# Odd chunks of a state-space kernel's scores with their source halves exchanged between the column halves of TensorE

## What is computed

```python
a = -jax.nn.softplus(A_log).transpose(0, 2, 1)
Lm = jnp.exp(segsum(a))                       # decay from s to l, zero for s > l
M = jnp.einsum('blhn,bshn,bhls->bhls', Cm, Bm, Lm)
y = jnp.einsum('bhls,bshp->blhp', M, x)
y = y + D[None, None, :, None] * x
out = y.reshape(b, l, D_INNER) * jax.nn.silu(z + z_bias) @ W_out.T
```

## Time and profile before

| | |
|---|---|
| median of three runs | 574.73 us |
| the three runs | 574.51, 574.73, 576.55 us |
| the profiled execution, its own time | 575.64 us |
| its span, first to last instruction | 573.9 us |
| TensorE / its weight loads / VectorE / ScalarE / GpSimd busy | 98% / 79% / 82% / 67% / 36% |

### The profile page before, as it was taken

How to read it: one execution, slowest core, us unless ns; L and a number is a source line. 1 busy time by engine, 2 the same in 40 slices (tenths; PEclk the granted TensorE clock), 3 DMA queues, 4 the chain that set the end, 5 groups by cost and what they waited for, 6 DMA issues and landing times.

```text
span 573.9 us, 18109 instructions
## 1 busy us (share of the span) xinstructions
PE 561.3 (98%) x6695; PEld 452.1 (79%) x6696; DVE 472.6 (82%) x753; ACT 387.3 (67%) x960; POOL 207.6 (36%) x377
## 2 busy tenths in 40 slices
PE   7899999999999999999999999999999999999997
PEld 4577787877787778777877878787678988989887
DVE  6899999899999989989999999999767648647343
ACT  1789888788788888877888887888544233323340
POOL 4852455463464464787245234426000000000000
PEclk9999999999999999999999999999999999999999
DMA  8545454433433435533343356546433043100101
GB/s 293 234 135 169 132 192 131 149 121 129 154 111 118 159 106 201 163 112 110 127 148 110 124 167 169 163 144 190 143 93 110 1 118 103 38 2 0 38 0 38
DMA packets 39660, 70.93 MB, mean 124 GB/s; under 512 B 4548, under 2 KB 10948, under 8 KB 39368
## 3 DMA queue, kind: packets, MB, share of 16 engines
q1 hardware_dynamic: 39624, 70.47, 38.3%
HBM read 57.34 MB, written 13.12 MB: 123 GB/s over the span
## 4 chain that ended last, share of the span: by engine, by line
PE 88%; DVE 6%; DMA 2%; issue 1%; POOL 1%; ACT 1%; SPq 0%; DVEq 0%; ACTq 0%; POOLq 0%
PE ps L336 18%; PE ps L338 18%; PE ps L337 18%; PE ps L505 11%; PE ps L549 5%; PE ps L488 5%; PE ps L540 4%; PE ps L524 4%; PE ps L615 2%; DVE acc L1104 2%; DVE acc L1016 1%; DMA wmod_sb<-in_wmod 1%; PE ps L358 1%; PE ps L561 1%; PE ps L388 1%
## 5 line engine op out<-in xcount | busy, mean ns | idle before, releaser
L1104 DVE SCALAR_TENSOR_TENSOR acc<-ps,cw_dve,acc 128x511 f32<-128x511 f32 (+2 forms) x384 | 259.2, 740 | 1.9 <-ACT acc L782 0.4
L814 ACT ACTIVATE decay<-sums,p_slot 128x128 f32<-128x128 f32 x512 | 160.7, 397 | 1.0 <-POOL sums L1380 0.2
L1380 POOL TENSOR_SCALAR_AFFINE_SELECT sums<-sums 128x512 f32<-128x512 f32 x128 | 82.4, 646 | 174.4 <-DMA sums<-running_sums 169.8
L782 ACT ACTIVATE acc<-ps,cw_act 128x512 f32<-128x512 f32 x128 | 93.1, 776 | 46.5 <-PE ps L549 44.4
L336 PE MATMUL ps<-ht_hi,wg_hi 128*128 128x512 f32 x256 | 106.9, 418 | 1.5 <-POOL wg_lo L1313 1.0
L338 PE MATMUL ps<-ht_hi,wg_lo 128*128 128x512 f32 x256 | 101.1, 395 | 0.0
L337 PE MATMUL ps<-ht_lo,wg_hi 128*128 128x512 f32 x256 | 101.0, 394 | 0.0
L1092 DVE TENSOR_TENSOR mix<-ps,decay 128x1024 f32<-128x1024 f32 x64 | 78.1, 1220 | 20.6 <-PE ps L505 19.3
L931 ACT ACTIVATE silu_sb<-ps 128x512 f32<-128x512 f32 x32 | 19.2, 599 | 77.3 <-PE ps L338 77.3
L505 PE MATMUL ps<-acc 64*64 64x64 f32 (+1 forms) x2048 | 69.8, 255 | 0.2 <-DVE acc L1104 0.2
L505 PEld LDWEIGHTS ps<-acc 64*64 64x64 f32 x2048 | 54.4, 132 | 9.1 <-issue 8.4
(11 more groups left out here) (136 smaller groups left out, 898.8 us busy)
## 6 DMA issues: line engine op xcount, KB each, us to landing
sums<-running_sums SPq DMA_DIRECT2D x128, 256.0 KB, 3.2
y_parts<-yt_sb SPq DMA_DIRECT2D x32, 256.0 KB, 2.0
wg_raw<-in_w_bc SPq DMA_DIRECT2D x8, 512.0 KB, 4.6
stage<-y_parts SPq DMA_DIRECT2D x16, 256.0 KB, 4.3
u_sb<-in_u SPq DMA_DIRECT2D x4, 512.0 KB, 6.3
stage<-in_w SPq DMA_DIRECT2D x1, 2048.0 KB, 16.3
x_channels<-acc SPq DMA_DIRECT2D x8, 256.0 KB, 2.3
ee<-decay_rows SPq DMA_DIRECT2D x8, 256.0 KB, 4.3
```

The source lines that it names most:

```text
L782: af(acc[:, b % 2, t, :], ps[:, PROJ_BANK[t], :], ACT.Identity, bias=cw_act[:, t, 1:2], scale=cw_act[:, t, 0:1]).then_inc(s[f"tap_a{t}"], 1)
L814: i = af(decay[:, j, c * P:(c + 1) * P], sums[:, j, c * P:(c + 1) * P], ACT.Exp, scale=-1.0, bias=p_slot[:, b * CH + c, j:j + 1])
L1104: stt(a[:, d:], ps[:, PROJ_BANK[t], 0:L - d], cw_dve[:, t, TAPS - 1 - d:TAPS - d], a[:, d:], ALU.mult, ALU.add).then_inc(s[f"taps{t}"], 1)
L1380: gp.affine_select(out=v, in_=v, compare_op=ALU.is_ge, fill=FAR, base=0, pattern=[[0, CH], [1, P]], channel_multiplier=-1).then_inc(s["mas ...
```

## The change

- The scores of odd chunks (c = 1, 3) write sources h = 0 to the column half 1 and h = 1 to the column half 0 (`at`). So in odd chunks source s stands on partition (s + 64) mod 128.
- Everything that is indexed by source partition in odd chunks follows. `p_transposes` makes the odd chunks' bias with two matmuls of 64 columns, one for each half. `mask` becomes two selects: one over all 512 columns, with the bound of odd chunks 64 higher, and a second, on partitions 0 to 63 of the odd chunks alone, which waits for the first. ScalarE waits for both (`masked` counts twice as fast). `own_x` becomes two copies, even chunks from `x_tok`, odd chunks from `x_swapped`, a copy of x with the halves exchanged.
- `x_swapped` lies in the memory of `gates`. Eight DMAs (`swap_halves`, two for each batch) fill it: batch 0 after the first four loads of sums, batch 1 before step (0, 1), batches 2 and 3 before step (0, 2). The four loads of the gates move from before step (0, 3) to behind the last step, ahead of the load of `u2`, and wait for the last `own_x`.

```diff
+            def swap_halves(b):
+
+                sp.wait_ge(s["xtok_ev"], 2 * (b + 1))
+                odd = x_tok[:, b * CH + 1:(b + 1) * CH:2, :]
+                for h in range(2):
+                    sp.dma_start(x_swapped[NS * (1 - h):NS * (2 - h), b], odd[NS * h:NS * (h + 1)]).then_inc(s[f"ld_xs{b}"], 16)
...
             step(0, 2, 0)
-            sp.wait_ge(s["st_gates"], 16)
-            for b in range(B):
-                sp.dma_start(gates[:, b].rearrange("p k d -> p (k d)"),
-                             gates_d[b:b + 1, :].to_broadcast([P, 2 * D])).then_inc(s["ld_gates"], 16)
             step(0, 3, 0)
...
             step(NG - 1, B - 1, NG - 1)
+            sp.wait_ge(s["st_gates"], 16)
+            sp.wait_ge(s["xs_done"], 2 * NG * B)
+            for b in range(B):
+                sp.dma_start(gates[:, b].rearrange("p k d -> p (k d)"),
+                             gates_d[b:b + 1, :].to_broadcast([P, 2 * D])).then_inc(s["ld_gates"], 16)
             sp.wait_ge(s["proj2"], NG * B)
             load(u2[:], u_b[0], "ld_res")
...
                 for c in range(CH):
-                    i = nc.tensor.transpose(ps[:, 7, c * P:(c + 1) * P], sums_t[:, c * P:(c + 1) * P], ident)
+                    if c % 2 == 0:
+                        nc.tensor.transpose(ps[:, 7, c * P:(c + 1) * P], sums_t[:, c * P:(c + 1) * P], ident)
+                    else:
+                        for h in range(2):
+                            i = mm(ps[NS * (1 - h):NS * (2 - h), 7, c * P:(c + 1) * P],
+                                   sums_t[:, c * P + NS * h:c * P + NS * (h + 1)], ident, start=True, stop=True)
...
-                            i = mm(ps[NS * h:NS * (h + 1), 2 + a, c * P + NS * h:(c + 1) * P],
+                            at = h if c % 2 == 0 else 1 - h
+                            i = mm(ps[NS * at:NS * (at + 1), 2 + a, c * P + NS * h:(c + 1) * P],
...
-                pe.wait_ge(s["xs_done"], q + 1)
+                pe.wait_ge(s["xs_done"], 2 * q + 2)
...
-                act.wait_ge(s["masked"], 4 * q + j + 1)
+                act.wait_ge(s["masked"], 8 * q + 2 * j + 2)
...
-                x = x_tok[:, b * CH:(b + 1) * CH, bass.ds(g * GC, GC)]
-                gp.tensor_copy(xs[:, b % 2, :, :, 0:HD], x.rearrange("p c (j e) -> p c j e", j=JH)).then_inc(s["xs_done"], 1)
+                even = x_tok[:, b * CH:(b + 1) * CH:2, bass.ds(g * GC, GC)]
+                odd = x_swapped[:, b, :, bass.ds(g * GC, GC)]
+                gp.tensor_copy(xs[:, b % 2, 0::2, :, 0:HD], even.rearrange("p c (j e) -> p c j e", j=JH)).then_inc(s["xs_done"], 1)
+                if isinstance(n, int) and n < B:
+                    pool.wait_ge(s[f"ld_xs{b}"], 32)
+                gp.tensor_copy(xs[:, b % 2, 1::2, :, 0:HD], odd.rearrange("p c (j e) -> p c j e", j=JH)).then_inc(s["xs_done"], 1)
...
-                v = sums[:, j, :].rearrange("p (c l) -> p c l", c=CH)
-                gp.affine_select(out=v, in_=v, compare_op=ALU.is_ge, fill=FAR, base=0, pattern=[[0, CH], [1, P]],
+                v = sums[:, j, :].rearrange("p (c e l) -> p c e l", c=2, e=2)
+                gp.affine_select(out=v, in_=v, compare_op=ALU.is_ge, fill=FAR, base=0, pattern=[[0, 2], [NS, 2], [1, P]],
                                  channel_multiplier=-1).then_inc(s["masked"], 1)
+                await_unit("masked", 8 * n + 2 * j + 1)
+                o = v[0:NS, :, 1, :]
+                gp.affine_select(out=o, in_=o, compare_op=ALU.is_ge, fill=FAR, base=-NS, pattern=[[0, 2], [1, P]],
+                                 channel_multiplier=-1).then_inc(s["masked"], 1)
```

More of the change, by code:

```diff
@@ L142, in adaln_ssm_ffn_kernel @@
         h2_lo = sb("h2_lo", [P, KT, L], F32R)
+        x_swapped = gates
         zeros = sums[:, 2, 0:L // 2].bitcast(BF16)
@@ L163, in adaln_ssm_ffn_kernel @@
         eps2 rs2 xn2_done lnT2 h32b_done h2hi_done h2lo_done up_mm silu_done hid_done hhi2 hlo2 down_mm out_mul
-        x2_done st_x0 st_x1 e_rows st_e st_y0 st_y1 ld_y0 ld_y1 ld_rows y_scaled ysum y_x
+        x2_done st_x0 st_x1 ld_xs0 ld_xs1 ld_xs2 ld_xs3 e_rows st_e st_y0 st_y1 ld_y0 ld_y1 ld_rows y_scaled ysum y_x
         """.split()
@@ L257, in _ @@
                 load_sum(0, 0, j, first=True)
+            swap_halves(0)
             store_x(2)
@@ L260, in _ @@
             load_group(1)
+            swap_halves(1)
             step(0, 1, None)
@@ L263, in _ @@
             sp.dma_start(e_d, e_rows).then_inc(s["st_e"], 16)
+            swap_halves(2)
+            swap_halves(3)
             step(0, 2, 0)
-            sp.wait_ge(s["st_gates"], 16)
-            for b in range(B):
-                sp.dma_start(gates[:, b].rearrange("p k d -> p (k d)"),
-                             gates_d[b:b + 1, :].to_broadcast([P, 2 * D])).then_inc(s["ld_gates"], 16)
             step(0, 3, 0)
```

## The result

The change makes the kernel slower: 581.02 us (median of 5 runs, 579.38 to 581.91) against 574.99 us of the kernel before (574.51 to 577.00), a ratio of 1.0097 with a 95% interval of 1.0079 to 1.0115. I had forecast 571.1 us, and a range that ends at 576.5. The profiled execution took 580.35 us, with a span of 578.6.

What follows compares the result with a forecast made beforehand. TensorE, busy 98%, was taken as the bound, tied to VectorE in a ring. Terms -6.7 + 0.9 + 0.4 + 1.5 + 0.3 = -3.6 us, from 574.73 to 571.1 us; range 567.0 to 576.5.

Steps and rivals of the forecast that it cites:

- The saving of a call: Each scores call on TensorE gets about 0.19 us shorter, 12.2 us in 64 calls if all shows.
- the ring of VectorE and TensorE: Scores, mix, taps and last projection form a closed 11.06 us loop; only one of two scores calls lies in it.
- the lengths of the steps: Looped steps fall from 11.05 to 10.86 us, by 0.19; steps outside VectorE's loop fall by 0.35.
- The rival that quadrants of a row half don't overlap: Scores quadrants don't run beside each other, so the exchange gains nothing: 577.1 us, chance 0.10.
- what GpSimd pays: Second select 0.35 us plus 0.19 wait: 0.54 a mask, between 0.44 and 0.83; free except in three places.
- Group changes 0 to 3, 0.4 in all: TensorE waits 0.1 to 0.4 us for the third weight split, the ring hiding some: 0.4 us in all.
- Group 4 to 5, 0.9: Masks delay the split weights after the butterflies; the two steps around this change lose 0.9 us against now.
- Front, 1.5: At the front of the last step, added masks and a copy delay y_add by 1.9 us, out_project by 1.5.
- 5 us are left: GpSimd, busy 6.0 of 11.04 us in a usual step, has 5 us left, so added selects cost nothing there.
- Late gates and u, 0.3: In the tail, gates late by up to 0.7 us and u by up to 1.5 cost 0.3, ends 0 and 1.5.
- The third rival: GpSimd becomes the bound where weights are split, at 0.83 us a mask: 577.2 us, slower, chance 0.14.
- My "nothing" for the eight DMAs: SP's eight added DMAs, 0.43 us each, cost nothing; at worst 1.7 us for those of batches 2 and 3.

Runs made afterwards that it cites:

- reordered pair: The reordered kernel, 570.20 us, and the kernel before in the same GpSimd and SyncE order without the exchange, 573.93 us.
- reordered kernel: Changed kernel, GpSimd/SyncE reordered: butterflies spread, splits before x scaling, second-half y work before third mask, gates early, group 7's other loads behind first sums: 570.20 us.
- experiment 6: Changed kernel with GpSimd's scaling of x (0.75 us) moved behind the splits of tiles 3 and 2 in steps with splits: 577.46 us.
- experiment 3: Changed kernel with 10 busy matmuls on TensorE before the weights of group 5 and 12 before the first out_project: 580.67 us.
- experiment 1: Changed kernel with the scores of odd chunks put back into their own column halves, the rest of the change kept: 584.59 us.

## Why the prediction was wrong

**Right.** The saving of a call (0.19 us), the ring of VectorE and TensorE that lets one call of two count, and the lengths of the steps, nearly: the step shown fell by 0.24, not 0.19. In the reordered pair, the exchange leads by 5.5 us at 388.64, and the lead has grown by 5.9 since the first step; I had 6.1 for 27 steps. That it ends at 3.7 us, the size of my -3.6, is chance: 0.7 of the lead go before the first out_project, and 1.3 behind it, with the low clock, for which I had no term. The rival that quadrants of a row half don't overlap is out: undoing the exchange lengthened a call back and cost 3.6 us. (The Trainium skill, "TensorE: Matmul & The Clock Gate", Part 3, has matmuls start and end in program order, and under that rule I had the exchange give nothing. These calls don't keep to it: they fell from 1.02 to 0.83 us.)

**Wrong: what GpSimd pays.** The second select takes 0.40 us and its wait 0.22 to 0.23, 0.62 a mask in place of 0.54 and inside my bounds. What failed is what I made of it in the places without cover. The terms against the change's profile, from the columns above and the same marks at the earlier changes of group:

- "Group changes 0 to 3, 0.4 in all": they lost 0.21, 0.62, 0.42 and 0.52, where each was to gain 0.2 to 0.3 as in the reordered kernel. That is 2.6 to 2.7 us. I had 0.1 to 0.4 us of wait for the third split at each, and let the ring hide some of it; TensorE waited 0.29, 0.57, 0.53 and 0.57 there, and the ring hid nothing.
- "Group 4 to 5, 0.9": the step lost 2.75, 2.9 to 3.0 with the missing gain. I counted the one mask ahead of the last butterfly as put later by 0.54, and called the cover of the steps before it enough. GpSimd's last waits for a sum before the split show otherwise, first of before, then of the change:

```profile
241.85 0.64 POOL L1380 TENSOR_SCALAR_AFFINE_SELECT sums<-sums 128x512 f32<-128x512 f32 x1 [3.60 <-DMA sums<-running_sums]
...
252.23 0.64 POOL L1380 TENSOR_SCALAR_AFFINE_SELECT sums<-sums 128x512 f32<-128x512 f32 x1 [2.27 <-DMA sums<-running_sums]
```

```profile
240.47 0.64 POOL L1404 TENSOR_SCALAR_AFFINE_SELECT sums<-sums 128x512 f32<-128x512 f32 x1 [0.47 <-DMA sums<-running_sums]
```

  Pauses of 3.60 and 2.27 us went to 0.47 and nothing: the masks and butterflies filled two steps, and the lag ran on into the split, while TensorE came 1.9 us sooner to ask for it.
- "Front, 1.5": from 388.64 to the first out_project the change lost 2.8.
- Group 7 had no term. One of its steps lost 1.1, 1.5 with the gain of 0.4 that it has in the reordered kernel, because a late first sum makes the mask critical: the cover "5 us are left" holds for a step on average, and not behind a late load. The load was late behind the last split, so this too is GpSimd's queue ahead of a split (experiment 6).
- "Late gates and u, 0.3": behind out_project another 1.8 were lost, where the late loads and the low clock lie over one another. The clock had no term and no rival. A wait of TensorE was priced as its length only.

Together that is 11.7 us of loss where I had 3.1. The profiled execution ended 4.7 behind, so about 7.0 us are left for the gain (with the shift of the start in it), where I had 6.7: the gain was sized rightly, and all of the miss lies in what GpSimd's queue, the late loads and the clock cost.

The third rival (GpSimd is the bound where weights are split, 577.2 us, 0.14) had the mechanism, and its own condition, from about 0.45 us a mask on, was met by my own estimate of 0.54. I should have given it the likeliest place. Its sizes are off as well: 1.1 us for a change of group is too much, 1.8 for the change 4 to 5 too little, and it misses 581 by the clock, group 7 and the tail.

My "nothing" for the eight DMAs of the swapped halves was left untested by a run of its own, but the steps of group 0, in which they are issued, gain 0.1 to 0.4 us each in the reordered kernel, so no loss shows there.

**What stays open.** How much the low clock at group 5 would cost alone was not separated: with it prevented, GpSimd bound there. Why the clock fell behind one wait of 1.69 us and not behind one of 1.67 is not settled by two profiles, and the length of the wait alone doesn't decide: in the execution of experiment 3 TensorE waited 2.09 us before the last scores and kept its clock.

```profile
413.49 0.90 PE L532 MATMUL ps<-acc 64*64 64x128 f32 x32 [2.09 <-DVE mix L1127]
...
412.00:414.00 2.00, 0.51 (x24) 0.54 (x28) 2.00 (x4) 0.43 (x1) 1.02 (x1) 1.00 1.04 282
```

## What to carry to other kernels

Where an engine with slack gets more work, don't ask how much slack it has on average, but list the instructions on it that another engine waits for, and add up what is queued ahead of each since the engine's last idle time. A DMA that waits for one of them belongs to the list. When such a change loses, move before you remove: 0.75 us of work put behind two splits gave 3.6 us, and reordering turned +1.0% into -1.0%. Where two late things end together, test them together; each alone shows nothing.

## What was not expected of the hardware

A wait of TensorE can cost more than its length. At waits of 1.69, 2.41, 2.61 and 3.34 us the granted clock went to 1.2 GHz for 3 to 10 us, sometimes before the wait was over (398 to 400 us above), and a first out_project of 3.7 us took 5.4 to 6.5. At waits of 1.40, 1.67 and 2.09 us it stayed at 2.4. Six matmuls of no use in a wait of 1.7 us gave 1.6 us back between two profiled executions, and 0.6 to 1.6 in the medians, as one compares. The kernel of experiment 1 had 10 us at the low clock in the execution that was profiled, and runs 5.8 us apart (583.59 to 589.42). A smaller select is not cheaper in proportion: a quarter of the elements, on half of the partitions, took 0.40 us against 0.64, and GpSimd's wait for its own result took another 0.22.
